# Fourth attention block: scores, maxima and exponentials by pairs of heads, differences on GpSimd alone

## The chip, the cores and the metric

The program runs on one core of one Trainium2 chip. Its five engines work side by side, each through its own list of instructions in order, and meet by semaphores: PE (TensorE, matrix products, with its weight loads shown as PEld), DVE (VectorE), ACT (ScalarE), POOL (GpSimd) and SP, which here only issues DMAs. The metric is the device time of one execution in microseconds. Before the change three runs gave 3109.22, 3110.50 and 3111.86 us, a median of 3110.5 us.

## What is computed

The reference is a stack of four layers, each an attention-like block and a feed-forward block with a layer norm behind each, on 8 sequences of 256 tokens with 256 features. The change touches only the attention of the fourth layer, a differential attention: 16 heads, each with two softmaxes of its own over the same keys, whose difference goes through a third softmax.

```python
q = _rope((x @ Wq).reshape(b, s, 16, 32)); k = _rope((x @ Wk).reshape(b, s, 4, 32)); v = ...
energy = einsum('bqhad,bkhad->bahqk', q.reshape(.., 16, 2, 16), k_repeated)        # a = 0, 1
energy = where(causal, -1e30, energy)
scores = softmax(energy / sqrt(16))
diff = scores[:, 0] - lam * scores[:, 1]              # lam: one number per head
diff = softmax(where(causal, -1e30, diff))
att = einsum('bhqv,bvhd->bqhd', diff, v)
att = att * rsqrt(mean(att * att, -1) + 1e-8) * rms_w * (1 - LAM_INIT)
return att.reshape(b, s, 256) @ Wo
```

## The kernel before

The block handles one sequence after the other, b = 0 to 7. The 16 heads are four groups r of four heads g. A *unit* is one softmax a of one group r: four heads of 256 queries in two blocks of 128 (t = 0, 1), the first against 128 keys, the second against 256, so 384 columns in each head. A sequence has NU = 8 units, i = 2r + a. Each engine has its own function `sequence`, a Python loop over slots i = 0 to 7 around a hardware loop over b; what stands in slot i of it for unit i, i-1, i-2 and so on is the software pipeline, and the order in which the calls stand is the order of the engine's list. No planner sets it.

The way of a unit i, with the names of the functions:

- PE `scores`: eight products on four row groups of the array, one for each head (line 1721, `tile_position=(32 * g, 0)`; each is recorded twice, so 16 in the trace), then eight products that add the causal mask (line 1725). Each head has a PSUM bank of its own, `S` is banks 0 to 3, and there is one `S`. So PE waits for `p_exp`, the end of the exponentials of unit i-1, before it begins.
- DVE `maxima`: four reductions over PSUM, two for heads 0 and 1, two for heads 2 and 3 (line 1961). After each two a count on `nm_ready`.
- ACT `exponentials`: eight exponentials with their row sums (line 1864); the last releases the next `scores`.
- DVE `ratios`, once for both units of a group: reciprocal of the sums and a factor for each row (lines 1968 to 1970).
- The difference of the two softmaxes, unnormalised, in place in `pr`: half of the heads (one of each two) on DVE by a fused multiply-add (`difference`, line 1979), the other half on POOL by a multiply and an add (lines 1826 and 1829). POOL also masks each group (line 1816). From here on the group's four heads are two halves of two heads, also called units (`part(i)`).
- DVE `second_maxima` in slot i+2 (lines 1989 and 1991: two reductions, then a small product into `nb2`), ACT `second` in the same slot (line 1881, four exponentials), counted on `p_ready`.
- PE `turn` in slot i+3: six transposes into banks 4 and 5 (line 1736). ACT `out_of_psum` (line 1872) and DVE `out_of_psum` (line 1997) copy one head each.
- PE `values` (lines 1748 and 1751) in slots 1, 3, 5, 7, DVE `values_out`, PE `turn_back`, DVE `take_output` (lines 2008 and 2009) in the slot after it.

Once in a sequence: POOL `squares` (line 1833), the norm of the heads' outputs on DVE (`norm_1`, `norm_2`: lines 2016, 2017, 81, nine Newton steps on lines 84, 86 and 88, line 2022), PE `turn_output` (line 1767), ACT `output` (line 1887), PE `project_output` (line 1775), DVE `output` and `measure` (line 108 and on).

The order of ACT's slot i is exponentials of unit i, copy out of PSUM, `second`; in slot 6 then `output`. The order of PE's slot is `scores`, `values` or `turn_back`, `turn`.

## Time and profile before

| | us |
|---|---|
| median of three runs | 3110.5 |
| the profiled execution | 3111.67 |
| its span, first to last instruction | 3109.9 |
| first scores of this block | 2115.24 |
| busy of DVE and ACT in 2117 to 2588, 471 us | 389.9, 352.0 |

Of the span 1.8 us lie around the profile's first and last instruction. Busy times of an engine say how full it is, not what it waits for: for that, the rows give in brackets the idle time of the engine ahead of an instruction and who ended it.

### The profile page before, as it was taken

To read this page: it belongs to the slowest core of one execution; us is meant where nothing else is said; L and a number is where in the kernel's file an instruction comes from. 1 tells how busy PE (TensorE), PEld (TensorE's weight loads), DVE (VectorE), ACT (ScalarE), POOL (GpSimd) and SP (SyncE) were. 2 spreads that over 40 slices of the span, in tenths; PEclk is the share of its full clock that TensorE was granted. 3 is DMA by queue.
4 is the path that set the end of the run, shared out by engine and by line. 5 is a ranking of instruction groups with operands and counts; after the bars stand their busy time and mean duration, and the time that the engine had idled before them with its cause. 6 is when DMAs were issued, how large, how long until landed. Compare 5 with 4: busy or idle time off the path is not lost. (4 is left out here: it accounts for less than half of the span.)

```text
span 3109.9 us, 43072 instructions
## 1 busy us (share of the span) xinstructions
PE 2608.6 (84%) x14256; PEld 1883.3 (61%) x14256; DVE 1858.5 (60%) x4295; ACT 1310.5 (42%) x3605; POOL 359.7 (12%) x392
## 2 busy tenths in 40 slices
PE   7988999889999999998698877796555654999997
PEld 5665544457776777677476665543443433877876
DVE  3665233445464555445645757546888886777777
ACT  4663455533443344334222132205777773332322
POOL 2440000000000000000121000003444440000000
PEclk9998999989999999999899888896777776999998
DMA  3002000000000000002000000100000003000000
GB/s 148 10 7 82 1 0 0 0 35 1 3 3 3 0 3 3 3 0 75 16 0 0 0 0 0 37 6 29 24 19 19 24 9 132 1 1 0 0 0 27
DMA packets 26415, 56.11 MB, mean 18 GB/s; under 512 B 3696, under 2 KB 22896, under 8 KB 24688
## 3 DMA queue, kind: packets, MB, share of 16 engines
q1 hardware_dynamic: 26352, 55.32, 4.8%
q8 instruction: 33, 0.54, 0.1%
q14 instruction: 30, 0.25, 0.0%
HBM read 39.59 MB, written 2.10 MB: 13 GB/s over the span
## 5 line engine op out<-in xcount | busy, mean ns | idle before, releaser
L1864 ACT ACTIVATE l3a_pr<-psum,l3a_nm 128x128 f32<-128x128 f32 (+1 forms) x512 | 207.1, 430 | 202.8 <-DVE l3a_nm L1961 202.8
L1721 PE MATMUL psum<-l3a_kr,l3a_qr 32*128 32x128 f32 (+1 forms) x1024 | 91.1, 491 | 180.3 <-ACT l3a_pr L1864 176.9
L108 DVE TENSOR_TENSOR x_sb<-psum,x_sb 128x512 f32 (+2 forms) x48 | 41.7, 868 | 235.2 <-PE psum L950 135.5
L757 DVE TENSOR_TENSOR l0f_hg<-l0f_sq,psum 128x512 f32<-128x512 f32 x128 | 87.8, 688 | 151.1 <-ACT l0f_sq L689 148.3
L1721 PEld LDWEIGHTS psum<-l3a_kr,l3a_qr 32*128 32x128 f32 x1024 | 51.5, 271 | 198.8 <-ACT l3a_pr L1864 186.3
L995 ACT ACTIVATE l1a_pr<-psum,l1a_nb,l1a_rq 128x128 f32<-128x128 f32 (+1 forms) x256 | 127.2, 509 | 87.2 <-DVE l1a_nb L1048 84.9
L1221 POOL TENSOR_TENSOR l1f_acc<-l1f_t 128x512 f32<-128x512 f32 x4 | 6.3, 1573 | 1334.3 <-DVE l1f_t L1284 1334.3
L2178 PE MATMUL psum<-l3f_x_hi,l3f_w_hi 128*128 x384 | 154.5, 402 | 6.6 <-DVE l3f_w_lo L2261 6.6
L2225 ACT ACTIVATE l3f_sg<-psum 128x512 f32<-128x512 f32 x96 | 57.3, 597 | 240.3 <-PE psum L2181 240.3
L1961 DVE TENSOR_REDUCE l3a_nm<-psum 128x2 f32<-128x256 f32 (+1 forms) x256 | 124.6, 548 | 53.9 <-PE psum L1725 53.9
L2179 PE MATMUL psum<-xT,l3f_w_hi 128*128 x384 | 152.9, 398 | 0.0
L2180 PE MATMUL psum<-l3f_x_hi,l3f_w_lo 128*128 x384 | 152.3, 397 | 0.0
L914 PE MATMUL psum<-l1a_kT,l1a_qT 128*128 128x128 f32 (+1 forms) x512 | 120.2, 359 | 20.9 <-ACT l1a_pr L995 14.0
L2192 PE MATMUL psum<-l3f_w_hi,l3f_h_hi 128*128 128x256 f32 x384 | 127.6, 332 | 7.9 <-DVE l3f_h_lo L2279 7.9
L1816 POOL TENSOR_TENSOR l3a_pr<-l3a_pr,w_l3a_mask 128x1024 f32<-128x1024 f32 x32 | 75.3, 2352 | 486.2 <-ACT l3a_pr L1864 486.2
L652 PE MATMUL psum<-l0f_hg,w_l0f_w 128*128 128x512 f32 x256 | 130.6, 593 | 0.8 <-DVE l0f_hg L757 0.8
L645 PE MATMUL psum<-l0f_xl,w_l0f_w 128*128 x256 | 130.6, 592 | 0.0
L1881 ACT ACTIVATE l3a_pr<-l3a_pr,l3a_nb,l3a_rec 128x128 f32<-128x128 f32 (+1 forms) x256 | 120.8, 581 | 3.8 <-DVE l3a_nb L1991 3.8
L885 PE MATMUL psum<-l1a_xc,w_l1a_q 128*128 128x256 f32 x512 | 122.4, 382 | 0.0
L687 ACT ACTIVATE l0f_relu<-psum 128x512 f32<-128x512 f32 x128 | 76.3, 596 | 108.8 <-PE psum L645 104.4
L867 PE MATMUL psum<-w_l1a_k,l1a_xc 128*128 128x512 f32 x256 | 112.8, 599 | 9.8 <-DMA l1a_xc<-xT 9.8
L891 PE MATMUL psum<-w_l1a_v,l1a_xc 128*128 128x512 f32 x256 | 120.3, 592 | 0.0
(424 smaller groups left out, 6942.2 us busy)
## 6 DMA issues: line engine op xcount, KB each, us to landing
w_l3f_all<-l3f_all_dram SPq DMA_DIRECT2D x1, 9216.0 KB, 25.7
l3a_qr<-l3a_q_all SPq DMA_DIRECT2D x32, 256.0 KB, 2.5
w_l0f_w<-l0f_w_dram SPq DMA_DIRECT2D x2, 2048.0 KB, 10.0
w_l1f_all<-l1f_all_dram SPq DMA_DIRECT2D x1, 2560.0 KB, 8.8
x_sb<-x_dram SPq DMA_DIRECT2D x1, 2048.0 KB, 8.5
l0a_xc<-xT SPq DMA_DIRECT2D x8, 256.0 KB, 2.5
w_l1a_q<-l1a_q_dram SPq DMA_DIRECT2D x1, 2048.0 KB, 7.9
w_l1a_k<-l1a_k_dram SPq DMA_DIRECT2D x1, 2048.0 KB, 13.5
```

The costliest lines, as they stand in the source:

```text
L645: mm(HB[e % 3], w["w1"][:, e, :], xl[:, chunk], start=True, stop=True).then_inc(h_ps, 1)
L652: mm(YL, w["w2"][:, e, :], hg[:, e % 2, :], start=(e == 0), stop=(e == E - 1)).then_inc(used, 1)
L885: last = mm(bank(2 + j % 2)[:, i * T:(i + 1) * T], w["q"][:, k, (2 * j + i) * HD:(2 * j + i + 1) * HD], xc[:, k, :], start=(k == 0), stop= ...
L995: last = nc.scalar.activation(pr[:, n % 2, i, s], S[n % 2][:, i, s], ACT.Exp, bias=nb[:, n % 2, t, i:i + 1], scale=rq[:, t, 2 * n + i:2 * ...
L1721: mm(S[:, g, t * P:t * P + (t + 1) * P], qr[rows, a, r, t * P:(t + 1) * P], kr[rows, a, 0:(t + 1) * P], start=(t == 0), stop=False, tile_p ...
L1864: last = nc.scalar.activation(pr[:, r, a, g, k], S[:, g, k], ACT.Exp, bias=nm[:, i % 2, g, t:t + 1], accum_out=sums[:, r, a, g, t:t + 1])
L1881: last = nc.scalar.activation(pr[:, r, 1, g, k], pr[:, r, 0, g, k], ACT.Exp, bias=nb2[:, r, g, t:t + 1], scale=rec[:, r, 0, g, t:t + 1])
L1961: last = nc.vector.tensor_reduce(nm[:, i % 2, 2 * pair:2 * pair + 2, t], S[:, 2 * pair:2 * pair + 2, t * P:t * P + (t + 1) * P], AX.X, ALU ...
L2178: mm(bk[e % 2], hi, x_hi[:, k, chunk], start=(k == 0), stop=False)
L2179: mm(bk[e % 2], hi, x_lo[:, k, chunk], start=False, stop=False)
L2180: mm(bk[e % 2], lo, x_hi[:, k, chunk], start=False, stop=(k == KD - 1))
L2192: mm(Y[:, t, :], h_hi[:, e % 2, tokens], hi, start=False, stop=False)
```

## The change

Scores, maxima and exponentials of a unit are each cut into two calls, pair 0 for heads 0 and 1 (banks 0 and 1) and pair 1 for heads 2 and 3 (banks 2 and 3). `p_exp` counts pairs, so the scores of a pair wait for the exponentials of the same pair of the unit before. On PE half of `turn` for an older unit stands between the two pairs. The difference is made by POOL for both heads of a unit, in instructions twice as wide. `ratios` moves from the end of DVE's odd slots to the slot after, behind pair 0's maxima. `second_maxima`, `second`, `turn`, `values`, `turn_back` and `take_output` come one slot later, and `norm_1`, `norm_2`, `turn_output` and ACT's `output` too. `maxima(b, i, pair)` is the body of the old loop over pairs, `difference` on DVE is removed, and the functions that come one slot later have their lag raised by one. The core of the diff:

```diff
-                def scores(b, i, opening):
+                def scores(b, i, pair, opening):
                     r, a = i // A, i % A
-                    if i == 0:
-                        pe.wait_ge(k_staged, b + 1)
-                    if a == 0:
-                        pe.wait_ge(q_staged[r], b * 16 + 16)
+                    if pair == 0:
+                        if i == 0:
+                            pe.wait_ge(k_staged, b + 1)
+                        if a == 0:
+                            pe.wait_ge(q_staged[r], b * 16 + 16)
                     if not (opening and i == 0):
-                        pe.wait_ge(p_exp, b * NU + i)
+                        pe.wait_ge(p_exp, 2 * (b * NU + i) - 1 + pair)
                     for t in range(TT):
-                        for g in range(G):
+                        for g in range(2 * pair, 2 * pair + 2):
                             rows = slice(32 * g, 32 * g + 32)
                             mm(S[:, g, t * P:t * P + (t + 1) * P], qr[rows, a, r, t * P:(t + 1) * P], kr[rows, a, 0:(t + 1) * P],
                                start=(t == 0), stop=False, tile_position=(32 * g, 0))
-                    for g in range(G):
+                    for g in range(2 * pair, 2 * pair + 2):
                         for t in range(TT):
                             last = mm(S[:, g, 2 * t * P:(2 * t + 1) * P], c["idb"], c["maskb"], start=False, stop=(t == TT - 1))
-                        if g % 2 == 1:
-                            last.then_inc(s_ps, 1)
-
-                def turn(b, i):
-                    s = b * NU + i - 3
-                    r, heads = (i - 3) // 2 % R, part(i - 3)
-                    pe.wait_ge(p_ready, s + 1)
-                    for j, copied in enumerate((pt_even, pt_odd)):
-                        pe.wait_ge(copied, s + 1)
-                        for k in range(3):
-                            last = nc.tensor.transpose(PT[j][:, k * P:(k + 1) * P], pr[:, r, 1, heads.start + j, k * P:(k + 1) * P], c["id"])
-                        last.then_inc(pt_ps, 1)
+                    last.then_inc(s_ps, 1)
...
+                def turn(b, i, j):
+                    s = b * NU + i - 4
+                    r, heads = (i - 4) // 2 % R, part(i - 4)
+                    if j == 0:
+                        pe.wait_ge(p_ready, s + 1)
+                    pe.wait_ge((pt_even, pt_odd)[j], s + 1)
+                    for k in range(3):
+                        last = nc.tensor.transpose(PT[j][:, k * P:(k + 1) * P], pr[:, r, 1, heads.start + j, k * P:(k + 1) * P], c["id"])
+                    last.then_inc(pt_ps, 1)
...
+                        turning = live(i, 4, opening, closing)
+                        done = i % 2 == 0 and live(i, 6, opening, closing)
                         if not closing:
-                            scores(b, i, opening)
-                        if i % 2 == 1 and live(i, 5, opening, closing):
-                            if i == 7 and not opening:
-                                pe.wait_ge(oT_ready, b)
+                            scores(b, i, 0, opening)
+                        if done:
                             values(b, i)
-                        if i % 2 == 0 and live(i, 6, opening, closing):
+                        if turning:
+                            turn(b, i, 0)
+                        if not closing:
+                            scores(b, i, 1, opening)
+                        if i == 7 and not opening:
+                            turn_output(b - 1)
+                        if turning:
+                            turn(b, i, 1)
+                        if done:
                             if i == 0:
                                 pe.wait_ge(z_ready, b)
                             turn_back(b, i, opening)
-                        if live(i, 3, opening, closing):
-                            turn(b, i)
-                        if i == 6 and not opening:
-                            turn_output(b - 1)
...
-                    r, g = i // 2, part(i).start + 1
+                    r, heads = i // 2, part(i)
                     if i % 2 == 0:
                         pool.wait_ge(ratio_ready, b * R + r + 1)
                         pool.wait_ge(masked, b * R + r + 1)
                     for t in range(TT):
                         k = slice(t * P, t * P + (t + 1) * P)
-                        last = nc.gpsimd.tensor_tensor(pr[:, r, 1, g, k], pr[:, r, 1, g, k], ratio[:, r, g, t:t + 1].broadcast_to((P, (t + 1) * P)), ALU.mult)
+                        last = nc.gpsimd.tensor_tensor(pr[:, r, 1, heads, k], pr[:, r, 1, heads, k], bc(ratio[:, r, heads, t], 2, (t + 1) * P), ALU.mult)
                     last.then_inc(scaled, 1)
                     pool.wait_ge(scaled, s + 1)
-                    nc.gpsimd.tensor_tensor(pr[:, r, 0, g, :], pr[:, r, 0, g, :], pr[:, r, 1, g, :], ALU.add).then_inc(dif_odd, 1)
+                    nc.gpsimd.tensor_tensor(pr[:, r, 0, heads, :], pr[:, r, 0, heads, :], pr[:, r, 1, heads, :], ALU.add).then_inc(dif_ready, 1)
...
-                def exponentials(b, i, opening):
+                def exponentials(b, i, pair, opening):
                     r, a = i // A, i % A
-                    if not opening:
+                    if pair == 0 and not opening:
                         act.wait_ge(pt_ps, b * NU * 2 + 4 * r - 12)
-                    for g in range(G):
-                        if g % 2 == 0:
-                            act.wait_ge(nm_ready, b * NU * 2 + 2 * i + g // 2 + 1)
+                    act.wait_ge(nm_ready, 2 * (b * NU + i) + pair + 1)
+                    for g in range(2 * pair, 2 * pair + 2):
                         for t in range(TT):
                             k = slice(t * P, t * P + (t + 1) * P)
                             last = nc.scalar.activation(pr[:, r, a, g, k], S[:, g, k], ACT.Exp, bias=nm[:, i % 2, g, t:t + 1],
                                                         accum_out=sums[:, r, a, g, t:t + 1])
                     last.then_inc(p_exp, 1)
...
-                            exponentials(b, i, opening)
+                            exponentials(b, i, 0, opening)
+                        if i == 7 and not opening:
+                            output(b - 1)
+                        if not closing:
+                            exponentials(b, i, 1, opening)
+                        if live(i, 4, opening, closing):
+                            out_of_psum(b, i, opening)
                         if live(i, 3, opening, closing):
-                            r = (i - 3) // 2 % R
-                            if not (opening and i - 3 < 4):
-                                act.wait_ge(av_ps, b * R + (i - 3) // 2 - 1)
-                            out_of_psum(b, i)
-                        if live(i, 2, opening, closing):
                             second(b, i)
-                        if i == 6 and not opening:
-                            output(b - 1)
...
+                    r = (i - 1) // 2 % R
+                    dve.wait_ge(p_exp, 2 * (b * NU + i))
...
-                    dve.wait_ge(dif_even, s + 1)
-                    dve.wait_ge(dif_odd, s + 1)
+                    s = b * NU + i - 3
+                    r, heads = (i - 3) // 2 % R, part(i - 3)
+                    dve.wait_ge(dif_ready, s + 1)
...
-                            maxima(b, i)
+                            maxima(b, i, 0)
+                        if i % 2 == 0 and live(i, 1, opening, closing):
+                            ratios(b, i)
+                        if i % 2 == 0 and live(i, 6, opening, closing):
+                            values_out(b, i)
+                        if i % 2 == 1 and live(i, 7, opening, closing) and i < 7:
+                            take_output(b, i)
+                        if not closing:
+                            maxima(b, i, 1)
                             if i == 7:
                                 stage_next(b)
-                        if live(i, 2, opening, closing):
-                            if i % 2 == 0:
-                                difference(b, i - 1)
-                            second_maxima(b, i)
-                        if live(i, 3, opening, closing):
-                            if not (opening and i - 3 < 4):
-                                dve.wait_ge(av_ps, b * R + (i - 3) // 2 - 1)
-                            out_of_psum(b, i)
-                        if i % 2 == 1 and live(i, 5, opening, closing):
-                            values_out(b, i)
-                        if i % 2 == 0 and live(i, 6, opening, closing):
-                            if i == 6 and not opening:
+                        if live(i, 4, opening, closing):
+                            out_of_psum(b, i, opening)
+                        if i == 7 and not closing:
+                            if not opening:
                                 dve.wait_ge(oT_ps, b)
                             take_output(b, i)
+                        if live(i, 3, opening, closing):
+                            second_maxima(b, i)
                         if not opening:
-                            if i == 5:
+                            if i == 6:
                                 norm_1(b - 1)
                                 norm_2(b - 1)
                             if i == 7:
                                 output(b - 1)
                                 dve.wait_ge(z_ready, b + 1)
                                 measure(nc, st, x_sb, mv, b * TT - TT, TT, lw)
-                        if i % 2 == 1 and not closing:
-                            ratios(b, i)
-                            difference(b, i - 1)
```

How the lists of PE and POOL change in a sequence's slots:

PE, one slot with values in it (an odd one), before. `l3a_kr,l3a_qr` are the scores, `cb_sb` the mask, `l3a_pt` the values, `cf_sb,l3a_pr` the transposes of `turn`, `cf_sb,w_l3a_q` those of `turn_back`.

```order
L1721 MATMUL psum<-l3a_kr,l3a_qr 128x128 x4
L1721 MATMUL psum<-l3a_kr,l3a_qr 128x256 x4
L1725 MATMUL psum<-cb_sb 128x128 x8
L1742 ISA
L1748 MATMUL psum<-l3a_pt,w_l3a_k 32x256 x4
L1751 MATMUL psum<-l3a_pt,w_l3a_k 32x128 x4
L1736 MATMUL psum<-cf_sb,l3a_pr 128x128 x6
```

PE, a slot with values in it (now an even one) after the change:

```order
L1721 MATMUL psum<-l3a_kr,l3a_qr 128x128 x2
L1721 MATMUL psum<-l3a_kr,l3a_qr 128x256 x2
L1725 MATMUL psum<-cb_sb 128x128 x4
L1740 ISA
L1747 MATMUL psum<-l3a_pt,w_l3a_k 32x256 x4
L1750 MATMUL psum<-l3a_pt,w_l3a_k 32x128 x4
L1735 MATMUL psum<-cf_sb,l3a_pr 128x128 x3
L1721 MATMUL psum<-l3a_kr,l3a_qr 128x128 x2
L1721 MATMUL psum<-l3a_kr,l3a_qr 128x256 x2
L1725 MATMUL psum<-cb_sb 128x128 x4
L1735 MATMUL psum<-cf_sb,l3a_pr 128x128 x3
```

The scores of pair 1 now stand behind three transposes of `turn`, and the other three behind them.

POOL, one group of heads in the loop, before:

```order
L1816 TENSOR_TENSOR l3a_pr<-l3a_pr,w_l3a_mask 128x4x2x128
L1826 TENSOR_TENSOR l3a_pr<-l3a_pr,l3a_ratio 128x128
L1826 TENSOR_TENSOR l3a_pr<-l3a_pr,l3a_ratio 128x256
L1829 TENSOR_TENSOR l3a_pr<-l3a_pr 128x384
L1826 TENSOR_TENSOR l3a_pr<-l3a_pr,l3a_ratio 128x128
L1826 TENSOR_TENSOR l3a_pr<-l3a_pr,l3a_ratio 128x256
```

and after the change:

```order
L1819 TENSOR_TENSOR l3a_pr<-l3a_pr,w_l3a_mask 128x4x2x128
L1829 TENSOR_TENSOR l3a_pr<-l3a_pr,l3a_ratio 128x2x128
L1829 TENSOR_TENSOR l3a_pr<-l3a_pr,l3a_ratio 128x2x256
L1832 TENSOR_TENSOR l3a_pr<-l3a_pr 128x768
L1829 TENSOR_TENSOR l3a_pr<-l3a_pr,l3a_ratio 128x2x128
L1829 TENSOR_TENSOR l3a_pr<-l3a_pr,l3a_ratio 128x2x256
```

The number of POOL's instructions stays, each difference instruction works on two heads.

From DVE's list the fused multiply-adds of line 1979 are gone, and between the two pairs' maxima stand the ratios and `values_out` in even slots, `take_output` in odd ones.

## Rows read from the trace of the kernel before

**Rows 1.** The page's costliest groups: busy and mean; idle before, releaser

```profile
L1864 ACT ACTIVATE l3a_pr<-psum,l3a_nm 128x128 f32<-128x128 f32 (+1 forms) x512 | 207.1, 430 | 202.8 <-DVE l3a_nm L1961 202.8
L1721 PE MATMUL psum<-l3a_kr,l3a_qr 32*128 32x128 f32 (+1 forms) x1024 | 91.1, 491 | 180.3 <-ACT l3a_pr L1864 176.9
```

**Rows 2.** The timeline, one unit: start, length, engine, line, idle before

```profile
2311.02 0.53 ACT L1872 ACTIVATE l3a_pt<-psum 128x384 f32<-128x384 f32 x1
2311.22 1.66 PE L1721 MATMUL psum<-l3a_kr,l3a_qr 32*128 32x128 f32 x16 [1.13 <-ACT l3a_pr L1864]
2311.39 1.89 ACT L1881 ACTIVATE l3a_pr<-l3a_pr,l3a_nb,l3a_rec 128x128 f32<-128x128 f32 x4
2313.45 1.95 DVE L1961 TENSOR_REDUCE l3a_nm<-psum 128x2 f32<-128x256 f32 x4 [0.22 <-PE psum L1725]
2314.51 0.37 ACT L1864 ACTIVATE l3a_pr<-psum,l3a_nm 128x128 f32<-128x128 f32 x1 [1.24 <-DVE l3a_nm L1961]
2317.69 0.53 ACT L1872 ACTIVATE l3a_pt<-psum 128x384 f32<-128x384 f32 x1
2317.89 1.66 PE L1721 MATMUL psum<-l3a_kr,l3a_qr 32*128 32x128 f32 x16 [2.94 <-ACT l3a_pr L1864]
```

**Rows 3.** PE's timeline: scores at both clocks, transposes, starts of sequences

```profile
2353.76 1.54 PE L1736 MATMUL psum<-cf_sb,l3a_pr 128*128 128x128 f32 x6
2356.43 0.94 PE L1721 MATMUL psum<-l3a_kr,l3a_qr 32*128 32x128 f32 x16 [1.14 <-ACT l3a_pr L1864]
2357.30 0.62 PE L1725 MATMUL psum<-cb_sb 128*128 128x128 bf16 x8
2358.55 0.87 PE L1736 MATMUL psum<-cf_sb,l3a_pr 128*128 128x128 f32 x6 [0.40 <-ACT l3a_pr L1881]
2362.79 1.67 PE L1721 MATMUL psum<-l3a_kr,l3a_qr 32*128 32x128 f32 x16 [3.37 <-ACT l3a_pr L1864]
...
2399.07 0.94 PE L1721 MATMUL psum<-l3a_kr,l3a_qr 32*128 32x128 f32 x16
2457.04 0.94 PE L1721 MATMUL psum<-l3a_kr,l3a_qr 32*128 32x128 f32 x16
```

**Rows 4.** Windows: length; busy of PE, PEld, DVE, ACT, POOL; clock, DMA

```profile
2117.00:2588.00 471.00, 276.19 (x2552) 186.66 (x2554) 389.94 (x983) 351.98 (x1351) 212.72 (x231) 0.73 0.05 18
2356.40:2358.40 2.00, 1.72 (x26) 1.15 (x26) 1.88 (x6) 2.00 (x5) 1.17 (x3) 1.00 0.00 0
2362.80:2365.00 2.20, 2.20 (x22) 1.55 (x23) 0.94 (x4) 2.05 (x5) 2.18 (x1) 0.50 0.00 0
```

**Rows 5.** PE's timeline of 2304.50 to 2304.75: how many scores had begun

```profile
2304.54 0.60 PE L1721 MATMUL psum<-l3a_kr,l3a_qr 32*128 32x128 f32 x4 [3.37 <-ACT l3a_pr L1864]
```

**Rows 6.** POOL's lines: L1829 by form; L374 shortest, median, longest in ns

```profile
L1829 POOL TENSOR_TENSOR l3a_pr<-l3a_pr 128x384 f32<-128x384 f32 x64 | 68.0, 1063 | 5.0
...
L374 POOL TENSOR_TENSOR l0a_pr<-l0a_pr,l0a_rec x128: 610/827/1044, 31.4 to 245.2; 128x256 f32<-128x256 f32 x64, 128x512 f32<-128x512 f32 x64
```

**Rows 7.** The timeline of POOL and DVE around 2322

```profile
2321.21 2.35 POOL L1816 TENSOR_TENSOR l3a_pr<-l3a_pr,w_l3a_mask 128x1024 f32<-128x1024 f32 x1
2323.03 0.55 DVE L1991 TENSOR_TENSOR l3a_nb<-l3a_nm,l3a_rec 128x4 f32<-128x4 f32 x1
```

**Rows 8.** DVE: line 1991 in another slot; the norm and what follows

```profile
2354.90 0.16 DVE L1991 TENSOR_TENSOR l3a_nb<-l3a_nm,l3a_rec 128x4 f32<-128x4 f32 x1
...
2324.31 0.67 DVE L2016 TENSOR_REDUCE l3a_vv<-w_l3a_q 128x32 f32<-128x512 f32 x1
2328.08 0.25 DVE L1968 RECIPROCAL l3a_rec<-l3a_sums 128x16 f32<-128x16 f32 x1
```

**Rows 9.** PE's timeline: values, the output projection at either clock

```profile
2320.45 0.90 PE L1748 MATMUL psum<-l3a_pt,w_l3a_k 128*32 128x256 f32 x8
...
2571.13 1.89 PE L1775 MATMUL psum<-l3a_wo,w_l3a_q 128*128 128x256 f32 x8
2597.14 3.78 PE L1775 MATMUL psum<-l3a_wo,w_l3a_q 128*128 128x256 f32 x8 [0.69 <-ACT w_l3a_q L1887]
```

More of the change, by code:

```diff
@@ L1843, in _ @@
                         difference(b + 1, i)
[L1844 removed]
+                        if i == 3:
                             squares(b)
@@ L1866, in exponentials, with out_of_psum @@
                     last.then_inc(p_exp, 1)
-                def out_of_psum(b, i):
-                    s = b * NU + i - 3
-                    r, g = (i - 3) // 2 % R, part(i - 3).start
+                def out_of_psum(b, i, opening):
+                    s = b * NU + i - 4
+                    r, g = (i - 4) // 2 % R, part(i - 4).start
+                    if not (opening and i - 4 < 4):
+                        act.wait_ge(av_ps, b * R + (i - 4) // 2 - 1)
                     act.wait_ge(pt_ps, 2 * s + 1)
@@ L1874, in second @@
                 def second(b, i):
-                    s = b * NU + i - 2
-                    r, heads = (i - 2) // 2 % R, part(i - 2)
+                    s = b * NU + i - 3
+                    r, heads = (i - 3) // 2 % R, part(i - 3)
                     act.wait_ge(nb_ready, s + 1)
@@ L1970, in ratios @@
                     nc.vector.tensor_tensor(ratio[:, r, :, :], ratio[:, r, :, :], bc(by_quad[:, r, :], 2, TT), ALU.mult).then_inc(ratio_ready, 1)
[L1972 to L1981 removed]
                 def second_maxima(b, i):
[L1984 to L1987 removed]
+                    s = b * NU + i - 3
+                    r, heads = (i - 3) // 2 % R, part(i - 3)
+                    dve.wait_ge(dif_ready, s + 1)
                     for t in range(TT):
@@ L1991, in second_maxima, with out_of_psum @@
                     nc.vector.tensor_tensor(nb2[:, r, heads, :], nm2[:, r, heads, :], rec[:, r, 0, heads, :], ALU.mult).then_inc(nb_ready, 1)
-                def out_of_psum(b, i):
-                    s = b * NU + i - 3
-                    r, g = (i - 3) // 2 % R, part(i - 3).start + 1
+                def out_of_psum(b, i, opening):
+                    s = b * NU + i - 4
+                    r, g = (i - 4) // 2 % R, part(i - 4).start + 1
+                    if not (opening and i - 4 < 4):
+                        dve.wait_ge(av_ps, b * R + (i - 4) // 2 - 1)
                     dve.wait_ge(pt_ps, 2 * s + 2)
```

43 lines of the change are left out of this document (13 added, 30 removed).

## The prediction

> **What bounds the kernel now.** I read the page's costliest groups first, then the timeline of a few units in the block, then the granted clock by windows. In [rows 1] the dearest group of ACT and the dearest group of PE in this block wait for each other: the exponentials wait 202.8 us for the maxima, the scores 180.3 us for the exponentials. That is one ring, since there is one set of PSUM banks: scores, maxima, exponentials, scores of the next unit. [Rows 2] has one turn of it. Scores start at 2311.22, maxima at 2313.45 (2.23 later), the first exponential at 2314.51 (1.06), and the next scores start at 2317.89, 0.05 behind the last of eight exponentials that take 3.33: 2.23 + 1.06 + 3.33 + 0.05 = 6.67 us for a unit. In the same turn ACT waits 1.24 us (between the end of line 1881 and the exponentials), so it has 5.43 us of work in 6.67. The ring has a second speed: in [rows 3] the scores take 0.94 us instead of 1.67 and the slot that starts at 2356.43 lasts 6.36 us (until 2362.79). [Rows 4] gives the reason: the granted clock is 1.00 (2.4 GHz) there and 0.50 (1.2 GHz) in the next slot, ahead of which PE sat idle for 3.37 us. A whole sequence, from 2399.07 to 2457.04 in [rows 3], takes 57.97 us, so its slots last 7.25 on the mean: those around the norm and the output projection are longer. There are eight sequences.
>
> **What the change does to the ring.** With p_exp counted by pairs, scores of one pair can run beside the exponentials of the other, which is meant to fill ACT's 1.24 us. But ACT, PE and DVE keep their lists in order, and on PE the first half of `turn` now stands between the scores of pair 0 and those of pair 1. That half waits for `p_ready` of the unit that ACT's `second` finished at the very end of the slot before. So for pair 1 a new ring closes, with every step in a row and nothing of it beside another:
> - exponentials of pair 1: eight take 3.18 from the first to the copy behind them (2314.51 to 2317.69 [rows 2]), so four 1.59;
> - ACT's copy, 0.37 until `second` starts, then `second`, 1.89 [rows 2];
> - 0.05 to PE, then three transposes. Six take 0.87 at full clock and 1.54 at half [rows 3], so three 0.44 or 0.77, with a little for the turn to the scores' tiling 0.5 or 0.9;
> - scores of pair 1 and four mask products until the maxima can start. Four heads need 0.87 until the mask begins and half of the mask's 0.62 [rows 3], with the signal 1.25; at half clock 2.23 as above. What two heads need is the disputed term. In [rows 5] four products on four row groups have begun within the first 0.21 us, so they run side by side; two at a time then last as long as four: 1.25 or 2.23. The other bound is half of the scores' part, 0.43 or 0.8 less, if it is issue that counts. I take the full value, since the recorded starts are together;
> - 1.06 for the maxima until ACT starts.
>
> Sum at full clock: 1.59 + 0.37 + 1.89 + 0.05 + 0.5 + 1.25 + 1.06 = 6.71; at half clock 1.59 + 0.37 + 1.89 + 0.05 + 0.9 + 2.23 + 1.06 = 8.09. ACT's idle time stays (6.71 - 5.43 = 1.28): the overlap won for pair 0 is spent on waiting for `second` and the transposes. Pair 0 is not late: its maxima end some 2.6 us after pair 1's exponentials start and ACT needs them at 3.8.
>
> The clock decides between the two. PE's work grows, since the scores run twice per unit with half the row groups in use, and its longest idle stretch in a slot shrinks from 3.37 us [rows 3] to about 2.9 (from the end of pair 0's scores at 1.0 to the transposes at 3.9, odd slots; in even slots `values` lies in it). I let the clock fall in one odd slot of three. Such a slot costs 8.09, and the even one behind it, in which `values` are late by a slow PE, some 7.4: 1.03 a slot over 6.71 on the mean. Six common slots: 6 x (6.71 + 1.03 / 3) = 42.3.
>
> **Parts at nothing.** The multiply-adds leave DVE (line 1979), but DVE is not on the new ring apart from its maxima. It is busy 389.9 of 471.0 us now [rows 4], 6.1 of each unit's 7.4, and only loses work, so it fits a slot of 6.7. `ratios` one slot later costs nothing: `second_maxima` also moves. POOL's instructions double in width. The scaling has its likeness in the first layer: 0.61 and 1.04 us [rows 6]. The add of 768 columns is not in the trace; 1.5 times the 1.04 of 512 columns is 1.56, twice 1.063 is 2.13; I take 1.9, nearer to the same instruction. Per group POOL has 2 x (0.61 + 1.04 + 0.08 + 1.9) + 2.35 = 9.6 us in two slots of 13.4 or more, and starts when the ratios come, 3.2 us into an even slot's share. So POOL does not bound (with 2.13, 10.1). It would if two slots fell under 10.
>
> **Where POOL's new width does cost.** In [rows 7] the product of line 1991, 0.16 us elsewhere [rows 8], starts at 2323.03 and ends at 2323.58, 0.02 after POOL's mask (2321.21 + 2.35 = 2323.56). It is so once in each full sequence. I take it that a DVE instruction with two operands in SBUF stands still while POOL works. The nine Newton steps, and line 2022, have two such operands, and in the old kernel they fall in POOL's gap. In the new one they come at 1.6 + 1.1 = 2.7 us after the start of pair 1's exponentials of slot 6, and POOL is busy with the second difference until 3.5 and with the mask until 5.9. The norm's 3.77 us (2324.31 to 2328.08 [rows 8]) would end at 5.4; so it ends at about 8.5, 3.1 later. The Trainium skill, page "SBUF — State Buffer", on the port pair that DVE and GpSimd share, says that it is an exclusive lock held for a whole instruction, also against a DVE instruction with two SBUF inputs when GpSimd reads SBUF. The trace agrees for line 1991; for the Newton steps no run here shows it. By the row alone, which is one small product, the norm might be let through, 3.1 us cheaper in each sequence; that is the second rival.
>
> Slot 7: the norm ends at 8.5, pair 0's maxima and exponentials follow (1.06 + 1.57), then ACT's `output`, 0.6, which now stands between the pairs, then pair 1: 11.8 us (8.7 unblocked). Slot 0: the output projection, 1.89 us at full clock, 3.78 at half [rows 9], stands ahead of the next scores on PE. After it come pair 0's scores (1.5 or 2.6 with their masks), `values` (about 1, [rows 9]), transposes 0.55, scores of pair 1 1.25, 1.06 to ACT: 1.95 + 1.5 + 1.05 + 0.55 + 1.25 + 1.06 = 7.4 at full clock, 3.85 + 2.6 + 1.05 + 0.55 + 1.25 + 1.06 = 10.4 if the clock is low until `values`. After PE's long wait in slot 7 I take 8.7, between them.
>
> **Sum.** A sequence: 42.3 + 11.8 + 8.7 = 62.8 against 57.97, +4.8; seven of them +33.6. The first one has no norm, and its first slots lack `second`: about -2. The end is one difference longer: +1. So +32.6 on the profiled execution's 3111.7 (span 3109.9 and 1.8 around it): 3144.3. The median lies 1.2 below that execution: 3143, of which I say 3142. Own range, by one odd slot in six to all of them at half clock and slot 0 at 7.4 to 10.4: 3125 to 3172.
>
> **Rivals.**
> - *As forecast, but PE keeps the full clock.* For it: the longest idle stretch shrinks. Against: 2.9 us is near the 3.37 ahead of a half-clock slot. 6 x 6.71 + 11.8 + 7.4 = 59.5, +10 over seven sequences, -1: 3119. The Trainium skill, page "TensorE: Matmul & The Clock Gate", Part 1, holds that the default is throttled and activity releases the throttle; the trace agrees, as the scores at 2356.43 ran at full clock behind transposes that had kept PE busy at half [rows 3], and those at 2362.79 at half behind 3.37 us of rest.
> - *The norm is not held up by POOL.* 42.3 + 8.7 + 8.7 = 59.7, +12 - 1: 3121.
> - *Both: full clock and free norm (faster side).* 40.3 + 8.7 + 7.4 = 56.4, -1.6 x 7 - 1: 3098. It is one place, the two slots around the norm, and decides from the point where slots 7 and 0 cost under 17.6 together at full clock.
> - *Two heads' scores cost half.* 0.43 less in each slot at full clock, with a free norm 3098 - 56 x 0.43 = 3074; with a held-up norm about the time of before. Against it: [rows 5].
> - *The pairs do what they are built for*: ACT at 5.43 a unit, 64 x (6.5 - 5.43) less than now, some 3045. It needs `second` to be done before PE reaches the transposes; by the lists it is not.
> - *Half clock throughout*: 6 x 8.09 + 11.8 + 12.2 = 72.5, +101: 3211. Against it: more work on PE than before.
>
> **How the numbers follow.** Forecast 0.46; full clock with held-up norm 0.12 (half of it within 0.2%); free norm 0.14; full and free 0.11; half-price scores 0.07; ACT-bound 0.04; half clock 0.06. Faster by over 0.2% (under 3104.3; about what a measurement of this kernel tells from no change): 0.11 + 0.07 + 0.04 = 0.22. Within: 0.06, and 0.02 from its neighbours, 0.08. Slower: 0.70. The range takes in the case at 3098 and leaves out the last three: 3090 to 3172.
>
> **What the profile after would show.** If right: on ACT one wait of about 1.3 us (2.6 at half clock) in each slot ahead of pair 1's exponentials and none ahead of pair 0's; pair 1's scores on PE directly behind transposes that waited for line 1885; scores of a pair as long as those of four heads, 0.94 or 1.66 us; Newton steps that last 2 us where POOL is busy; slot 7 at 11 to 12 us. Wrong if the wait is ahead of pair 0, if a pair's scores take 0.5 us at full clock, or if the slots of a sequence sum to under 58 us.

## The result and the profile after

Before 3111.2 us (4 runs), after 3207.3 us (3205.5 to 3210.1, 4 runs): ratio 1.031, 95% interval 1.0292 to 1.0328. The forecast was 3142, range 3090 to 3172. The direction was right, and 65 us are missing. The profiled execution took 3206.8, its span 3205.0 against 3109.9.

The page after, columns as in [rows 1]:

```profile
L1866 ACT ACTIVATE l3a_pr<-psum,l3a_nm 128x128 f32<-128x128 f32 (+1 forms) x512 | 208.1, 421 | 278.6 <-DVE l3a_nm L1963 278.1
L1721 PE MATMUL psum<-l3a_kr,l3a_qr 32*128 32x128 f32 (+1 forms) x1024 | 204.4, 547 | 8.5 <-ACT l3a_pr L1866 4.3
L1735 PE MATMUL psum<-cf_sb,l3a_pr 128*128 128x128 f32 x384 | 108.7, 421 | 85.2 <-ACT l3a_pr L1885 85.1
```

The exponentials work as long as before (208.1 against 207.1) and wait longer (278.6 against 202.8). The scores no longer wait for them, but are busy for 204.4 us instead of 91.1, and the transposes of `turn` now wait 85.2 us, nearly all of it for the second exponentials (line 1885); before it was 7.8 (line 1736). The timeline of PE and ACT, two slots after the change, columns as in [rows 2]:

```profile
2409.27 1.65 PE L1721 MATMUL psum<-l3a_kr,l3a_qr 32*128 32x128 f32 x8
2412.03 1.65 PE L1721 MATMUL psum<-l3a_kr,l3a_qr 32*128 32x128 f32 x8
2414.71 1.08 PE L1747 MATMUL psum<-l3a_pt,w_l3a_k 128*32 128x256 f32 x8 [0.49 <-ACT l3a_pt L1876]
2416.45 0.90 PE L1735 MATMUL psum<-cf_sb,l3a_pr 128*128 128x128 f32 x3 [0.24 <-ACT l3a_pr L1885]
2417.28 1.65 PE L1721 MATMUL psum<-l3a_kr,l3a_qr 32*128 32x128 f32 x8
2420.47 1.65 PE L1721 MATMUL psum<-l3a_kr,l3a_qr 32*128 32x128 f32 x8
2424.84 0.90 PE L1735 MATMUL psum<-cf_sb,l3a_pr 128*128 128x128 f32 x3 [2.18 <-ACT l3a_pr L1885]
2425.67 1.65 PE L1721 MATMUL psum<-l3a_kr,l3a_qr 32*128 32x128 f32 x8
...
2404.16 0.37 ACT L1866 ACTIVATE l3a_pr<-psum,l3a_nm 128x128 f32<-128x128 f32 x1 [2.56 <-DVE l3a_nm L1963]
2406.53 1.86 ACT L1885 ACTIVATE l3a_pr<-l3a_pr,l3a_nb,l3a_rec 128x128 f32<-128x128 f32 x4 [0.27 <-DVE l3a_nb L1981]
2412.56 0.37 ACT L1866 ACTIVATE l3a_pr<-psum,l3a_nm 128x128 f32<-128x128 f32 x1 [2.57 <-DVE l3a_nm L1963]
```

Pair 1's scores start at 2409.27, 2417.28 and 2425.67: slots of 8.01 and 8.39 us in turn. (A slot is here counted from the start of pair 1's scores to the next.) Each stands right behind transposes that waited for line 1885, and takes 1.65 us for two heads, as four did [rows 2]. ACT waits 2.56 us ahead of pair 1 alone. This is the ring that was forecast, at its half-clock price. The windows, columns as in [rows 4]:

```profile
2117.00:2588.00 471.00, 376.71 (x2158) 229.66 (x2154) 287.94 (x712) 301.24 (x1153) 254.37 (x196) 0.52 0.05 18
2378.00:2390.00 12.00, 12.00 (x66) 7.30 (x65) 6.68 (x20) 5.94 (x24) 4.97 (x5) 0.50 0.00 0
2317.60:2522.00 204.40, 166.15 (x915) 101.87 (x914) 124.83 (x312) 130.43 (x496) 110.30 (x85) 0.50 0.05 17
2310.80:2317.40 6.60, 5.42 (x58) 3.22 (x56) 5.46 (x19) 2.69 (x12) 1.87 (x3) 1.00 0.00 0
```

The granted clock of the block is 0.52 (before 0.73) although PE is busy for 376.7 us of 471 instead of 276.2. In the second window, around the start of a sequence, PE has 12 us of work without a gap, at 0.50 (1.2 GHz) all along; 2.5 us of it are the output projection over all 128 rows, the rest scores, masks, `values` and transposes. The third window is 204 us long and wholly at 0.50. Full speed came back three times between 2117 and 2588, each time at the end of the projection or right behind it, and was lost within 7 us; the fourth window is one of the three. Around the norm and the start of the next sequence:

```profile
2433.68 1.65 PE L1721 MATMUL psum<-l3a_kr,l3a_qr 32*128 32x128 f32 x8
2436.97 0.37 ACT L1866 ACTIVATE l3a_pr<-psum,l3a_nm 128x128 f32<-128x128 f32 x1 [2.56 <-DVE l3a_nm L1963]
...
2439.93 1.70 DVE L2009 TENSOR_SCALAR l3a_vv<-l3a_vv 128x32 f32<-128x32 f32 x1
2441.66 0.18 DVE L81 TENSOR_SCALAR l3a_rs<-l3a_vv 128x32 int32<-128x32 int32 x1
...
2439.24 2.34 POOL L1819 TENSOR_TENSOR l3a_pr<-l3a_pr,w_l3a_mask 128x1024 f32<-128x1024 f32 x1
...
2442.08 1.65 PE L1721 MATMUL psum<-l3a_kr,l3a_qr 32*128 32x128 f32 x8
2447.92 3.75 PE L1774 MATMUL psum<-l3a_wo,w_l3a_q 128*128 128x256 f32 x8 [1.51 <-ACT w_l3a_q L1891]
2455.99 1.65 PE L1721 MATMUL psum<-l3a_kr,l3a_qr 32*128 32x128 f32 x8
```

One small instruction of the norm is held until the mask ends, the nine Newton steps run free. From slot 7's pair 1 (2442.08) to slot 0's (2455.99) go 13.91 us, 11.8 to 12.3 where full speed came back at the projection. A sequence from 2442.08 to the same point at 2513.21 lasts 71.1 us; over the six from 2232.11 to 2653.68 it is 70.3 on the mean, against 57.97.

### The profile page after: what moved, and what is told of

The parts are those of the page before. It is cut to its first block and busy times, and to the rows that moved or that the text cites. A ratio compares the mean times of both kernels' runs of the same rounds, so it can differ in the third digit from the quotient of the medians.

```text
span 3205.0 us, 42765 instructions
## 1 busy us (share of the span) xinstructions
PE 2778.8 (87%) x14256; PEld 1968.9 (61%) x14256; DVE 1811.6 (57%) x4167; ACT 1316.0 (41%) x3605; POOL 445.8 (14%) x392
## 5 line engine op out<-in xcount | busy, mean ns | idle before, releaser
L1866 ACT ACTIVATE l3a_pr<-psum,l3a_nm 128x128 f32<-128x128 f32 (+1 forms) x512 | 208.1, 421 | 278.6 <-DVE l3a_nm L1963 278.1
L1721 PE MATMUL psum<-l3a_kr,l3a_qr 32*128 32x128 f32 (+1 forms) x1024 | 204.4, 547 | 8.5 <-ACT l3a_pr L1866 4.3
L1735 PE MATMUL psum<-cf_sb,l3a_pr 128*128 128x128 f32 x384 | 108.7, 421 | 85.2 <-ACT l3a_pr L1885 85.1
L1721 PEld LDWEIGHTS psum<-l3a_kr,l3a_qr 32*128 32x128 f32 x1024 | 115.4, 308 | 50.6 <-issue 46.1
L1829 POOL TENSOR_TENSOR l3a_pr<-l3a_pr,l3a_ratio 128x256 f32<-128x256 f32 (+1 forms) x128 | 103.2, 828 | 237.4 <-DVE l3a_ratio L1972 237.4
L1735 PEld LDWEIGHTS psum<-cf_sb,l3a_pr 128*128 128x128 f32 x384 | 66.9, 216 | 107.0 <-ACT l3a_pr L1885 104.8
```

Source lines behind the costliest of these rows:

```text
L1721: mm(S[:, g, t * P:t * P + (t + 1) * P], qr[rows, a, r, t * P:(t + 1) * P], kr[rows, a, 0:(t + 1) * P], start=(t == 0), stop=False, tile_p ...
L1735: last = nc.tensor.transpose(PT[j][:, k * P:(k + 1) * P], pr[:, r, 1, heads.start + j, k * P:(k + 1) * P], c["id"])
L1866: last = nc.scalar.activation(pr[:, r, a, g, k], S[:, g, k], ACT.Exp, bias=nm[:, i % 2, g, t:t + 1], accum_out=sums[:, r, a, g, t:t + 1])
```

## The experiments

Each was timed in three rounds beside the kernel before, whose median was 3110.25 to 3111.65. Clock is the granted clock of 2117 to 2588.

### Which part of the change costs

**GpSimd alone makes the differences, all else as before.**

```diff
+ pool: difference on both heads (mult 128x2x128, 128x2x256, add 128x768)
- dve:  difference(b, i - 1)
```

> The kernel before with one part of the change alone: all differences on GpSimd for both heads, nothing else. Theory, that this part costs next to nothing, or gives back what the fused multiply-adds held up of the maxima: 3095 to 3112 us. Rival, that GpSimd is then late for the second maxima in even slots and its lock holds up the norm: 3125 us or more.

3112.6 us, ratio 1.0007 (0.9997 to 1.0016): nothing. GpSimd's add took 1.81 us. The trace shows that this nothing is a balance. Slots 1 to 5 of a sequence last 31.5 us instead of 32.8 (mean of six sequences, scores to scores), and slots 6, 7 and 0, around the norm and the projection, 26.4 instead of 25.5. The clock of the block is 0.70.

**Scores of all four heads in one piece, all the rest as changed.**

```diff
- scores(b, i, 0, opening) ... scores(b, i, 1, opening)
+ scores(b, i, opening)          # waits for both pairs, ahead of values and turn
```

> The changed kernel with the scores of a unit in one piece again, four heads on four row groups, all else as changed (differences all on GpSimd, later steps one slot on). Theory, that the split of the scores is what costs (two heads as dear as four, a second ring, and PE at the lower clock): mean granted clock of the block back from 0.52 to about 0.75, slots of 6.4 to 6.7, 3100 to 3120 us. Rival, that GpSimd's wider differences, which hold up small VectorE products, cost a good part: 3140 to 3170 us.

3147.3 us, ratio 1.0120 (1.0103 to 1.0137), clock 0.69. The time lies in the range of the rival, not of the theory. All that the change does besides the split of the scores, above all the later steps, harmless by my working, costs 37 us. DVE at the norm, and the projection behind it:

```profile
2344.47 0.96 DVE L2007 TENSOR_SCALAR l3a_vv<-l3a_vv 128x32 f32<-128x32 f32 x1
2345.68 1.68 DVE L84 TENSOR_TENSOR l3a_tmp<-l3a_rs 128x32 f32<-128x32 f32 x1
2347.39 2.26 DVE L86 SCALAR_TENSOR_TENSOR l3a_tmp<-l3a_vv,l3a_tmp 128x32 f32<-128x32 f32 x1
...
2352.92 0.37 ACT L1864 ACTIVATE l3a_pr<-psum,l3a_nm 128x128 f32<-128x128 f32 x1 [7.19 <-DVE l3a_nm L1961]
2355.27 3.75 PE L1774 MATMUL psum<-l3a_wo,w_l3a_q 128*128 128x256 f32 x8 [1.51 <-ACT w_l3a_q L1889]
```

Three instructions of 0.18 or 0.19 us stand still here, each for one of GpSimd's; the norm takes 8.1 us instead of 3.8 [rows 8], and ACT waits 7.19 us behind it. The projection runs at half clock in every sequence (3.75 us); before the change it took 1.89 in the seven inside the loop [rows 9]. The loss lies around the norm: slots 6, 7 and 0 last 30.0 us instead of 25.5, slots 1 to 5 32.9 instead of 32.8.

**Values and both halves of turn behind pair 1's scores.**

```diff
                             scores(b, i, 0, opening)
+                            scores(b, i, 1, opening)
                         if done: values(b, i)
                         if turning: turn(b, i, 0)
-                            scores(b, i, 1, opening)
                         if turning: turn(b, i, 1)
```

> The changed kernel with both halves of the transposes behind pair 1's scores on PE (values too). Ring theory: pair 1's scores no longer wait for ACT's second exponentials, so the 8.2 us slot (mean of 8.40 and 8.01) falls to what PE or ACT hold. At half clock PE has about 7.1 us of work in a slot: about 3207 - 56 x 1.1 = 3145 us. If the clock also comes up, ACT's 5.5 us bind and the time goes to about 3060. Rival, that the low clock alone costs the time and the order on PE does not matter: 3200 to 3210.

3128.3 us, ratio 1.0058 (1.0041 to 1.0074), clock 0.64. So of the 97 us, 79 belong to what stood between the two pairs on PE (the first half of `turn`, which the forecast's ring runs through, and `values`), with the clock that came back with it. Cut into pairs without that, the scores win 19 us over four heads in one piece.

### Why the clock stayed low

**A filler over the whole array, ahead of pair 0's scores, and its control on 32 rows.**

```diff
+ for x in range(16): mm(S[:, 0, 0:P], idb, maskb)                     # first: 128 rows
+ for x in range(16): for g in range(2): mm(S[:, g, 0:P], idb[32g..], maskb[32g..], tile_position=(32 * g, 0))   # second
```

> The changed kernel with 16 extra products of the full array (128 rows, 128 columns, bf16) ahead of pair 0's scores in every slot, into the bank that these then overwrite. They add 1.7 us of PE work at half clock, 0.9 at full, mostly in PE's idle time. Theory, that PE stays at the lower clock since its time is filled by products on two of four row groups: the clock rises from 0.52 to 0.8 or more and the kernel gets faster in spite of more work, 3130 to 3160 us. Rival, that work of any kind does not lift it while ACT's waits set the rhythm: 0.5 stays and the time is 3207 to 3235 us.

> The changed kernel with 16 pairs of bf16 products ahead of pair 0's scores, each pair side by side on 32 rows of the array (row groups 0 and 1), into a bank that is overwritten afterwards. It is the control to the filler of 16 products that used all 128 rows: same place, same number of steps, same time on PE. Theory (what kind of work it is decides: products on two row groups do not bring the clock back): the granted clock of the block stays at 0.50 to 0.56 and the time is 3207 to 3240 us. Rival (any work that fills PE's idle stretches raises the clock, or the filler of 128 rows helped by its time alone): clock 0.70 or more, time near the 3190 us of that filler.

First 3190.5 us (1.0258, 1.0241 to 1.0275), second 3233.9 (1.0395, 1.0372 to 1.0417). The windows, first the one, then the other:

```profile
2117.00:2588.00 471.00, 368.08 (x3156) 264.16 (x3153) 300.68 (x740) 311.66 (x1195) 263.01 (x203) 0.75 0.05 18
```

```profile
2117.00:2588.00 471.00, 408.34 (x3766) 279.88 (x3765) 280.46 (x674) 291.36 (x1110) 243.80 (x189) 0.59 0.05 16
```

With more work on PE the kernel is 17 us faster in the first and 27 slower in the second. The clock goes to 0.75 with whole-array products and to 0.59 with those on two row groups, which take PE as long (1.07 us at full clock against 1.06, 1.89 at half against 1.91). The kind of work matters most; filling alone does something too, so neither theory holds in its pure form. Both fillers are bf16: whether fp32 products over all rows would help as much was not tried.

The first filler also settles what the clock is worth. In two of the seven sequences behind the first, pair 1's scores ran at full clock in all six common slots:

```profile
2249.42 0.93 PE L1724 MATMUL psum<-l3a_kr,l3a_qr 32*128 32x128 f32 x8
2256.13 0.92 PE L1724 MATMUL psum<-l3a_kr,l3a_qr 32*128 32x128 f32 x8
...
2269.69 0.92 PE L1724 MATMUL psum<-l3a_kr,l3a_qr 32*128 32x128 f32 x8
...
2289.88 0.92 PE L1724 MATMUL psum<-l3a_kr,l3a_qr 32*128 32x128 f32 x8
```

From 2249.42 to 2289.88, six slots, go 40.46 us, where the forecast's 6 x 6.71 makes 40.3 and the changed kernel takes 48.8. Where its clock is low, a slot costs 8.86 or 9.23 us instead of 8.01 or 8.39, with 1.9 us more to do on PE; that is how a block at 0.75 can still take 3190 us.

**Before, score products in the order of pairs.**

```diff
- for t in range(TT): for g in range(G):
+ for pair in range(2): for t in range(TT): for g in range(2 * pair, 2 * pair + 2):
```

> The kernel before the change, with nothing changed but the order of the eight score products in a unit: first the four of heads 0 and 1, then the four of heads 2 and 3, so that two run side by side instead of four. The ring, the waits and all other work stay. Theory (work on two row groups does not hold or bring back the clock): the scores take 1.85 us at full clock and 3.3 at half, the granted clock of the block falls from 0.73 to under 0.6, and nearly all slots cost 1.65 us more than a half-clock slot of 6.67: some 64 times 1.7 more on the mean of 6.5, so 3110 + 110 = 3220 us (3190 to 3235). Rival (the clock goes by how full PE is, and PE becomes fuller by this): the clock stays at 0.70 or rises, 64 times 0.92 more: 3169 us (3150 to 3180).

3109.7 us, ratio 0.9996 (0.9986 to 1.0005). My premise failed, so this says nothing on the clock: eight products still take 0.95 us in the new order. What fits all the rows is that each row group goes through its own two products and the groups overlap in either order; two heads then last as long as four.

```profile
2308.59 0.95 PE L1721 MATMUL psum<-l3a_kr,l3a_qr 32*128 32x128 f32 x16 [1.13 <-ACT l3a_pr L1864]
2314.95 1.68 PE L1721 MATMUL psum<-l3a_kr,l3a_qr 32*128 32x128 f32 x16 [3.37 <-ACT l3a_pr L1864]
```

**Before, scores in two pieces with each pair's mask products behind it.**

```diff
+ for pair in range(2):
+     products of heads 2 * pair, 2 * pair + 1; their masks; s_ps + 1
```

> The kernel before the change, with the scores of a unit in two pieces as the changed kernel has them: products of heads 0 and 1, their mask products, products of heads 2 and 3, their mask products. The mask products use all rows of the array and stand between, so the two pairs cannot run beside each other. Everything else stays as before, the ring over all four heads too. The extra time of PE is mostly hidden: pair 1's maxima are 0.3 us early at full clock and 0.5 us late at half. Theory (the pieces, not the new order of the slots, take the clock): the granted clock of the block falls from 0.73 to 0.6 or less, and the time is 3110 + 56 x 0.7 = 3149 us (3135 to 3165). Rival (the clock goes by how full PE is): the clock stays at 0.70 or over, 3110 to 3126 us.

3166.5 us, ratio 1.0179 (1.0162 to 1.0196). PE and the window:

```profile
2352.28 1.65 PE L1722 MATMUL psum<-l3a_kr,l3a_qr 32*128 32x128 f32 x8 [4.18 <-ACT l3a_pr L1864]
2354.40 1.65 PE L1722 MATMUL psum<-l3a_kr,l3a_qr 32*128 32x128 f32 x8
2361.64 0.92 PE L1722 MATMUL psum<-l3a_kr,l3a_qr 32*128 32x128 f32 x8
```

```profile
2117.00:2588.00 471.00, 343.76 (x2342) 221.92 (x2340) 353.60 (x889) 327.12 (x1251) 194.87 (x210) 0.65 0.05 18
```

The kernel before loses clock (0.73 to 0.65, I had said 0.60) by the two pieces alone, while PE grows busier by 68 us. The rival, by which the clock goes by how full PE is, falls. Why the pieces cost clock is not shown. My reading is that only half of the array works in each; running products on the other two row groups beside them would test it, and was not tried.

**Whole-array products in PE's own wait, off the ring.**

```diff
+ for x in range(18 if i % 2 == 1 else 2): mm(PT[0][:, 0:P], idb, maskb)
  pe.wait_ge(p_ready, s + 1)
```

> The changed kernel with bf16 products over all 128 rows in PE's own wait for the second exponentials: 18 in odd slots (1.9 us at half clock in a wait of 2.2), 2 in even slots, into a bank that the transposes overwrite. At half clock they lie beside ACT's work and lengthen nothing. Theory (in this order of work the clock alone makes 8.2 us of a slot that takes 6.7 at full clock): the granted clock of the block rises from 0.52 to 0.65 or more, and each slot at full clock is worth 1.4 us: 3207 - 15 to 45 = 3177 us (3160 to 3192). Rival (the products of the pairs throttle whatever stands between them): clock under 0.56, 3203 to 3212 us.

3190.9 us, ratio 1.0253 (1.0236 to 1.0270), clock 0.63. Pair 1's scores of three slots:

```profile
2401.56 0.92 PE L1721 MATMUL psum<-l3a_kr,l3a_qr 32*128 32x128 f32 x8
...
2408.27 1.62 PE L1721 MATMUL psum<-l3a_kr,l3a_qr 32*128 32x128 f32 x8
...
2416.82 1.65 PE L1721 MATMUL psum<-l3a_kr,l3a_qr 32*128 32x128 f32 x8
```

The windows of the first and of the second slot:

```profile
2401.60:2408.20 6.60, 4.21 (x49) 2.56 (x48) 4.45 (x12) 4.96 (x20) 1.13 (x2) 1.00 0.00 0
2408.50:2416.80 8.30, 8.03 (x50) 5.56 (x50) 4.87 (x10) 5.67 (x23) 6.67 (x7) 0.50 0.20 70
```

The slot that began at full clock lasts 6.71 us, to the hundredth the forecast's full-clock ring, and the granted clock is 1.00 all through it; the next, at 0.50, lasts 8.55. A higher clock with fillers that stand only in PE's wait gives 16 us back. It did not last through the slots here, as it did in two sequences of the run with 16 products ahead of pair 0.

### The norm and GpSimd

**Changed kernel, and four heads in one piece, each with the last mask behind the norm.**

```diff
  pool.wait_ge(p_exp, 2 * (b * NU + 2 * r + 1))
+ if r == 3 and b > 0: pool.wait_ge(on_ready, b)
```

> The changed kernel in which POOL's mask of the last group of heads waits until the norm of the sequence before is done; nothing needs it earlier, since its difference waits for ratios of the next slot. Theory (the mask holds up the norm's first small instructions by 1.5 us and nothing else): the norm takes 3.8 us instead of 5.3, slot 7 is 1.5 us shorter, 3197 us (3193 to 3201). Rival 1 (the hold-up stands beside PE's and ACT's other waits): no change, 3204 to 3210. Rival 2 (the forecast's 3.1 us a sequence): 3186.

3195.7 us, ratio 1.0274 (1.0257 to 1.0291): 11.6 us, 1.66 a sequence, as the theory of 1.5 said. Line 2011 (2009 in the changed kernel) takes 0.18 us again:

```profile
2438.77 0.18 DVE L2011 TENSOR_SCALAR l3a_vv<-l3a_vv 128x32 f32<-128x32 f32 x1
```

> The version with the scores of four heads in one piece and all the rest as in the changed kernel (3147 us), with POOL's mask of the last group behind the norm. In that version three small DVE instructions of the norm are held: 0.96 us (line 2007), 1.68 (line 84) and 2.26 (line 86), by POOL's scaling, add and mask one after the other. Theory: the third goes, 2.1 us in each of seven sequences, 15 us: 3132 us (3128 to 3137), and the other two stay. Rival (DVE's hold-ups stand beside another wait): 3144 to 3150.

3140.9 us, ratio 1.0093 (1.0077 to 1.0110): 6.4 instead of 15. Line 86 is free (0.19), 2.1 us less a sequence on DVE, but under half of it reaches the end: slots 6, 7 and 0 last 28.1 us instead of 30.0, slots 1 to 5 33.3 instead of 32.9. Of the other 30 us, the projection at half clock, 1.9 us in each of seven sequences, makes about 13 by my estimate; the rest was not taken apart.

### Towards a faster kernel

**As turn last, with values_out behind pair 1's maxima on DVE.**

```diff
-  maxima 0, ratios, values_out, maxima 1
+  maxima 0, ratios, maxima 1, values_out
```

> The version with values and both halves of turn behind pair 1's scores (3128 us), and with DVE's values_out behind pair 1's maxima instead of ahead of them. There ACT waits 1.4 to 1.9 us in each even slot for pair 1's maxima, which stand behind values_out, which waits for values on PE. Theory: this wait goes, 4 a sequence of about 1.4 us, less what PE's half clock then takes back (an even slot has 7.9 us of PE work at half clock, an odd one 5.7, and ACT 5.4): 3095 us (3080 to 3112). Rival (PE at half clock is the bound, 13.6 us for two slots against 12.7 now): no gain, 3122 to 3135.

3113.2 us, ratio 1.0012 (1.0003 to 1.0022), clock 0.67: 15 us won of 33 hoped for. It lies outside both ranges, just above the theory's.

**In addition slot 7 in another order.**

```diff
  PE:   turn 0, turn 1, turn_output, project_output     (turn_output stood between)
  ACT:  exponentials 0, 1, out_of_psum, output          (output stood between)
  DVE:  maxima 0, maxima 1, norm_1, norm_2, ...         (the norm stood in slot 6)
  POOL: last mask behind the norm
```

> As the run before (values_out late), with the slot around the norm put in another order: maxima of both pairs of slot 7 stand ahead of the norm on DVE, turn_output stands behind the transposes on PE, ACT's output behind both pairs' exponentials, and POOL's mask of the last group waits for the norm. Theory: ACT's 5.7 us wait in slot 7 becomes exponentials done beside the norm; the projection (3.75 us at half clock) stays in the path: some 3 us a sequence, 20 us less than the run before, 3075 us (3060 to 3095). Rival (slot 7 still ends with the norm, the projection at half clock and the maxima in a row, so what is won ahead of the norm is waited for behind it): within 5 us of the run before.

3103.9 us, ratio to before 0.9979 (0.9970 to 0.9989): below before by 0.2%, the only version that is. Of the 20 us by which it was to beat the run before, 9 came. One wait is left at the start of a sequence:

```profile
2440.29 3.56 PE L1774 MATMUL psum<-l3a_wo,w_l3a_q 128*128 128x256 f32 x8 [0.78 <-ACT w_l3a_q L1893]
2444.01 0.69 DVE L108 TENSOR_TENSOR x_sb<-psum,x_sb 128x512 f32 x1 [2.81 <-PE psum L1774]
2447.66 0.37 ACT L1868 ACTIVATE l3a_pr<-psum,l3a_nm 128x128 f32<-128x128 f32 x1 [4.56 <-DVE l3a_nm L1965]
```

**In addition the projection in slot 0 of the next sequence.**

```diff
  PE slot 0:  scores 0, scores 1, project_output(b - 2), values, ...
  DVE slot 0: maxima 0, ratios, maxima 1, output(b - 2), values_out, measure
```

> The version with turn last, values_out late and slot 7 reordered (3104 us), with the output projection on PE and the add and the statistics of the output on DVE moved from the end of slot 7 into slot 0 of the sequence after it, behind both pairs' scores and maxima (one sequence on PE and DVE stands ahead of the loop for that). Theory: ACT's wait of 4.6 us at the start of each sequence (projection 3.6 us at half clock, scores, statistics, maxima in a row) goes and one of about 2 us comes back behind it, since the projection now delays the values and the scores of slot 1: 3087 us (3075 to 3098). Rival (PE at half clock is the bound, so the projection costs its 3.6 us wherever it stands): within 5 us of 3104.

3120.4 us, ratio 1.0020 (1.0006 to 1.0034); eight of ten runs lay at 3119.5 to 3122.1 with a mean clock of 0.899 or 0.900, two at 3105.0 and 3105.3 with 0.908 and 0.909. So even its better runs only reach the 3103.9 us of the run before, and the longer time goes with the lower clock. Both forecasts missed. In the profiled execution, one of the eight, the block's clock was 0.62 (0.66 in the run before). Slot 7 lasts 10.3 us instead of 13.5 on the mean of six sequences, slots 0 and 1 15.9 instead of 12.3, and slots 2 to 6 32.4 instead of 31.3: what the projection no longer costs in slot 7 it costs in the two slots behind.

## Why the prediction failed, by its own steps

- **The new ring for pair 1** was right in its place, its steps and its price: 6.71 at full clock (measured 6.71), 8.09 at half (8.01 and 8.39). Term by term the full-clock slot of the run with products in PE's own wait agrees within 0.05 us. Every second slot is 0.38 longer: line 1981's small product stands still until GpSimd's add ends, 0.94 us instead of 0.16, and ACT's `second` waits for it. That was not in the sum.
- **Two heads' scores as long as four**: right, 0.92 and 1.65 us. The forecast took it from starts that lie together; two products in a row on each row group fit the runs too.
- **"I let the clock fall in one odd slot of three"** is the step that failed. It stayed low in nearly all slots. Six common slots took 48.8 us (71.1 less the 22.3 of slots 7 and 0, 2433.68 to 2455.99) instead of 42.3, and 48.8 to 49.9 in all seven sequences: some 47 us of the 65. With full clock they take 40.46, as the first filler showed, so it is the clock and not another wait.

  I read the clock off PE's idle stretches alone. The longest in a common slot shrank further than I said, in nearly all of them to 2.2 us instead of 2.9, and the clock stayed low all the same. I argued "more work on PE than before" against the case of half clock throughout, 3211 us, which had 0.06. That it came within 4 us is partly luck: a sequence lasts 70.3 us, not its 72.5, and the block's first and last part cost some 9 us more than before (my estimate from the span), where every sum of the forecast took 1 us off.

  The pieces alone take 0.08 of the clock (0.73 to 0.65), the order with turn between the pairs 0.12 (0.64 to 0.52), and of the 0.04 of the four-head version (0.73 to 0.69) GpSimd's part alone takes 0.03 (0.70). What in the pieces and the order does it stays open. The Trainium skill, page "TensorE: Matmul & The Clock Gate", Part 1, says that activity releases the throttle; read as any busy stretch, that does not fit the 12 us without a gap at 0.50, and the measurement decides.
- **The norm held up by 3.1 us**: one instruction was held, 1.5 us more than free, and the nine Newton steps ran after the mask. That GpSimd stops small DVE instructions was right, and not only those with two inputs: line 2009 has one. The Trainium skill, page "SBUF — State Buffer", "SBUF: two separate sides", states the lock for a whole instruction and names, beside two inputs in SBUF, a two-port mode of DVE; line 2009 ends 0.05 behind the mask, as by such a lock, and in which mode it runs no trace shows. I had the right mechanism and the mask too late: it ended 4.6 us after the start of pair 1's exponentials (2436.97 to 2441.58), not 5.9.
- **Slots 7 and 0** took 22.3 instead of 20.5 us in the sequence shown, 21.3 on the mean of six. Counted at pair 1's exponentials, slot 7 took 10.7 (said 11.8, with a norm held for longer) and slot 0 11.6 (said 8.7, and 10.4 at most, since I gave PE full clock behind `values`; it had half). Two errors partly cancel here.
- **GpSimd's add** 1.81 (said 1.9), and its doubled width at nothing: right, shown by the run that has it alone. **"`ratios` one slot later costs nothing"**, and with it the other later steps, was wrong in the four-head version, which takes 37 us more than before; how much of that is in the changed kernel is open.

## What to carry to other kernels

When an engine's list is cut into finer pieces for overlap, look at what stands between the pieces: one wait there joins two rings into one, and with the clock that it took cost 79 us here. Work out every case at both clocks and do not let a fuller TensorE stand for a faster one; ask what kind of work the new pieces are. Small DVE steps that other engines wait for are best put where GpSimd is idle, by making GpSimd wait for them where nothing needs its result.

## What the runs showed of the hardware

- TensorE kept 1.2 GHz through 12 us without a gap in scores on two row groups, transposes, masks, `values` and the output projection, and through 204 us in which it was busy for 166. 16 whole-array bf16 products a slot raised the block's clock to 0.75, as many pairs on 32 rows to 0.59.
- Products on different row groups overlap in any order of issue: at full clock eight took 0.94 us, or 0.95 in the order of pairs, and four 0.92.
- GpSimd held DVE instructions of 0.18 or 0.19 us on 128x32 for 0.96 to 2.26 us, one after the other, each until GpSimd's own ended; a TENSOR_SCALAR with one input too.
- One kernel (that of the last experiment) had two levels, 3105 and 3120 us, with mean clocks of 0.908 to 0.909 and 0.899 to 0.900.
